# Twelve attention batches: the loop over batches written out, and two value buffers that change roles

## The reference

```
# level 0: q and k normalised per head, then rotated;  softmax over the 4096 keys
# level 1: a bias by the distance of key and query;     softmax over the 4096 keys
# level 2: softmax over the 256 queries, then each query's weights divided by their sum over the keys
k, v = heads(context @ Wk), heads(context @ Wv)          # per batch: 16 heads x 4096 x 16
att  = softmax(q @ k.T * scale (+ bias))                 # 16 heads x 256 x 4096
x    = x + (att @ v).reshape(256, 256) @ Wo
```

## Time and profile before

| | |
|---|---|
| Median of 3 runs | 7475.54 us (7468.15 to 7477.53) |
| Profiled execution, its own time | 7475.55 us |
| Its span | 7473.7 us |
| PE, DVE, ACT, POOL busy | 81%, 57%, 44%, 14% of the span |
| Mean granted TensorE clock | 0.898 |
| Instructions | 103657 |

### The profile page before, as it was taken

One profiled execution on the slowest core, in us unless ns is written; L12 is line 12 of the kernel. 1 busy time (PEld: TensorE's weight loads), 2 busy tenths in 40 slices (PEclk: granted clock), 3 DMA queues, 4 the chain that ended last, 5 costly groups with the idle time before them and its releaser, 6 DMA issues. The chain is left out here.

```text
span 7473.7 us, 103657 instructions
## 1 busy us (share of the span) xinstructions
PE 6076.2 (81%) x35500; PEld 3371.3 (45%) x35500; DVE 4251.5 (57%) x8502; ACT 3271.1 (44%) x7854; POOL 1056.2 (14%) x1131
## 2 busy tenths in 40 slices
PE   6798898979288369898898897878777898987887
PEld 3343443423155245454445554333333565556754
DVE  8677787839311236565573332888877444534631
ACT  3566565520033125454453111989889224532211
POOL 4222222004332320000000002111000000001100
PEclk8899998979599689999998998999988777998998
DMA  3323222130288433222210113322321000022100
GB/s 110 90 73 91 75 84 65 55 105 0 88 258 259 129 113 82 69 74 79 66 50 29 36 36 97 96 83 78 94 65 56 11 0 6 0 76 67 49 21 24
DMA packets 281192, 549.50 MB, mean 74 GB/s; under 512 B 29726, under 2 KB 186789, under 8 KB 261909
## 3 DMA queue, kind: packets, MB, share of 16 engines
q1 hardware_dynamic: 262388, 493.46, 22.2%
q0 software_dynamic: 18336, 50.09, 1.8%
HBM read 414.73 MB, written 128.75 MB: 73 GB/s over the span
## 5 line engine op out<-in xcount | busy, mean ns | idle before, releaser
L2413 DVE TENSOR_REDUCE t<-banks 128x1 f32<-128x512 f32 x2048 | 1373.1, 690 | 369.2 <-PE banks L2296 301.9
L2501 ACT ACTIVATE t<-banks 128x1024 f32<-128x1024 f32 x1024 | 1043.7, 1024 | 786.8 <-PE banks L2325 781.9
L2739 ACT ACTIVATE t<-banks,t 128x256 f32<-128x256 f32 x2048 | 938.1, 513 | 70.0 <-DVE t L2676 51.5
L2296 PE MATMUL banks<-t 96*128 96x512 bf16 x2048 | 798.9, 395 | 208.7 <-PEq L66 91.6
L2676 DVE TENSOR_REDUCE t<-banks 128x4 f32<-128x1024 f32 x512 | 623.7, 1219 | 92.2 <-PE banks L2622 53.0
L2342 PE MATMUL banks<-t 128*17 128x256 f32 x8192 | 642.2, 385 | 20.7 <-ACT t L2501 17.5
L2325 PE MATMUL banks<-t 97*128 97x256 bf16 x4096 | 650.6, 273 | 0.0
L2325 PEld LDWEIGHTS banks<-t 97*128 97x128 bf16 x4096 | 390.3, 98 | 256.3 <-issue 111.6
L2296 PEld LDWEIGHTS banks<-t 96*128 96x128 bf16 x2048 | 198.6, 97 | 659.7 <-DVE t L2413 336.4
L2739 ACT ACTIVATION_READ_ACCUMULATOR t<-banks,t 128x1 f32 x2048 | 494.4, 245 | 0.0
L2635 PE MATMUL banks<-t 128*17 128x256 f32 x4096 | 328.9, 407 | 160.9 <-DVE t L2687 108.1
(11 more groups left out here) (424 smaller groups left out, 10155.9 us busy)
## 6 DMA issues: line engine op xcount, KB each, us to landing
t<-in_L_ffn_w SPq DMA_DIRECT2D x127, 640.0 KB, 5.6
scratch_k<-t SPq DMA_DIRECT2D x192, 384.0 KB, 14.4
t<-scratch_k SPq DMA_DIRECT2D x192, 384.0 KB
t<-in_ctxT SPq DMA_DIRECT2D x128, 512.0 KB, 15.5
t<-scratch_k SPq DMA_DIRECT2D x192, 256.0 KB
t<-scratch_k SPq DMA_DIRECT2D x192, 128.0 KB
t<-in_L_ffn_w SPq DMA_DIRECT2D x18, 1024.0 KB
t<-in_c_rope_k SPq DMA_DIRECT2D x32, 512.0 KB, 16.6
```

The source lines that it names most:

```text
L2296: mm = nc.tensor.matmul(ps[:, 4 + g % 2, :], qstack[0:SHIFT, h, t * P:(t + 1) * P], kstack[0:SHIFT, h % 3, kc * KC:(kc + 1) * KC], start=T ...
L2413: nc.vector.tensor_reduce(gm[:, h % 2, g // NK, g % NK:g % NK + 1], ps[:, 4 + g % 2, :], AX.X, ALU.max).then_inc(max_done, 1)
L2501: nc.scalar.activation(p[:, i % 3, :].rearrange("p (b t) -> p b t", b=2), ps[:, 2 * (i % 2):2 * (i % 2) + 2, :], ACT.Exp).then_inc(exp_don ...
L2739: nc.scalar.activation(p[:, i % SL, j * T:(j + 1) * T], ps[:, 2 * (i % 3) + j // 2, (j % 2) * T:(j % 2 + 1) * T], ACT.Exp, bias=nm[:, i % ...
```

## The change

The loop is a Python loop, so that the body is emitted three times with constant batch numbers. The two buffers are a list, batch `b` reads `values[b % 2]` and fills `values[(b + 1) % 2]`, and the copy, with its part of each of the three engines, is gone from `output_product`.

```diff
-def output_product(core, att, attT, wo, b, moved=None, first=None):
+def output_product(core, att, attT, wo, b, first=None):
...
             nc.scalar.copy(attT[:, :, :], ps[:, 0:CT, 0:T]).then_inc(copied, 1)
-            if moved:
-                nc.scalar.copy(moved[1][:, CUT:CUT2], moved[0][:, CUT:CUT2])
-
-        if moved:
-            @block.gpsimd
-            def _(pool):
-                nc.gpsimd.tensor_copy(moved[1][:, CUT2:], moved[0][:, CUT2:])
 
         @block.vector
         def _(dve):
-            if moved:
-                nc.vector.tensor_copy(moved[1][:, 0:CUT], moved[0][:, 0:CUT])
             for t in range(QT):
...
-        v, v_next, kstack = sb([P, KT, H, VW]), sb([P, KT, H, VW]), sb([P, 3, S], BF16)
+        values, kstack = [sb([P, KT, H, VW]) for _ in range(2)], sb([P, 3, S], BF16)
...
-            project_first(core, wq, queries, q_rope, scale, wk, wv, context(0), keys[0], v, k_rope)
+            project_first(core, wq, queries, q_rope, scale, wk, wv, context(0), keys[0], values[0], k_rope)
...
-        of_batch = lambda b: (queries[:, :, :, bass.ds(b * T, T)].rearrange("s d h n -> (s d) h n"), keys[b], q97, k97)
+        of_batch = lambda b: (queries[:, :, :, b * T:(b + 1) * T].rearrange("s d h n -> (s d) h n"), keys[b], q97, k97)
 
         def attend_batch(b, coming):
             if by_key:
-                attend_by_key(core, keys[b], v, q97, k97, att, coming)
+                attend_by_key(core, keys[b], values[b % 2], q97, k97, att, coming)
             else:
-                attend_context(core, keys[b], v, q97, k97, tiles, att, coming)
-            output_product(core, att, attT, wo, b, (v_next, v) if coming else None, of_batch(b + 1) if coming else None)
+                attend_context(core, keys[b], values[b % 2], q97, k97, tiles, att, coming)
+            output_product(core, att, attT, wo, b, of_batch(b + 1) if coming else None)
...
-        with nc.Fori(0, B - 1) as b:
-            attend_batch(b, dict(w=wk, w_v=wv, v=v_next, source=context(b + 1), dest=keys[b + 1], rope=k_rope))
+        for b in range(B - 1):
+            attend_batch(b, dict(w=wk, w_v=wv, v=values[(b + 1) % 2], source=context(b + 1), dest=keys[b + 1],
+                                 rope=k_rope))
         attend_batch(B - 1, None)
```

More of the change, by code:

```diff
@@ L2517, in _ @@
                         new.low_parts(pool, u)
-def output_product(core, att, attT, wo, b, moved=None, first=None):
+def output_product(core, att, attT, wo, b, first=None):
     nc, ps = core.nc, core.ps
     QT = T // P
-    CUT, CUT2 = KT // 2, KT * 13 // 16
     with phase(core, "turned", "copied", "ready", "landed") as (block, turned, copied, ready, landed):
@@ L2775, in context_attention @@
             layer_norm(core, core.x, core.xn, core.xnT, loads=loads + [(wq[:, :, :], ktiles(d[prefix + "_Wq"]))],
-                       constants=[(kstack[SHIFT:ROWS, :, :], 1.0), (v[:, :, :, D:VW], 1.0), (v_next[:, :, :, D:VW], 1.0)]
+                       constants=[(kstack[SHIFT:ROWS, :, :], 1.0), (values[0][:, :, :, D:VW], 1.0),
+                                  (values[1][:, :, :, D:VW], 1.0)]
                        + ([(eps[:, :], 1e-6)] if rope else []))
-            project_first(core, wq, queries, q_rope, scale, wk, wv, context(0), keys[0], v, k_rope)
+            project_first(core, wq, queries, q_rope, scale, wk, wv, context(0), keys[0], values[0], k_rope)
         qstack, att, attT = sb([P, H, T], BF16), sb([P, T // P, C]), sb([P, CT, T])
         k97, q97 = kstack[0:ROWS], qstack[0:ROWS]
-        of_batch = lambda b: (queries[:, :, :, bass.ds(b * T, T)].rearrange("s d h n -> (s d) h n"), keys[b], q97, k97)
+        of_batch = lambda b: (queries[:, :, :, b * T:(b + 1) * T].rearrange("s d h n -> (s d) h n"), keys[b], q97, k97)
         def attend_batch(b, coming):
             if by_key:
-                attend_by_key(core, keys[b], v, q97, k97, att, coming)
+                attend_by_key(core, keys[b], values[b % 2], q97, k97, att, coming)
             else:
-                attend_context(core, keys[b], v, q97, k97, tiles, att, coming)
-            output_product(core, att, attT, wo, b, (v_next, v) if coming else None, of_batch(b + 1) if coming else None)
+                attend_context(core, keys[b], values[b % 2], q97, k97, tiles, att, coming)
+            output_product(core, att, attT, wo, b, of_batch(b + 1) if coming else None)
         with phase(core, "landed") as (block, landed):
```

## The result

The changed kernel takes 7447.66 us at the median of ten runs (7439.03 to 7456.25); the kernel before took 7468.54 beside it (ten runs, 7455.94 to 7477.53). The ratio is 0.9973, with a 95% interval of 0.9964 to 0.9982: some 20 us faster, between 13 and 27. The profiled execution took 7456.25 us, span 7454.4, and is the longest of its ten.

A forecast was written before the change was run, and what follows sets the result against it. No engine's work but transfers, then PE's taken branch, were held to set the boundaries between batches. Branches 9.0, earlier issue 3.0, last batches 0.4 and copy 0 gave 12.4 us off 7475.55: 7463, range 7451 to 7474.

The forecast's parts named there:

- The starting point: Whole kernel: the gain was taken off the profiled execution's 7475.55 us, with the median of the runs at 7475.54.
- The copy at nothing: Output phases between batches: the copy lies under the transfers, so removing it gains 0 us.
- The branches: Loop ends: nine branches go, six of them taken; batches 1 and 2 become as long as batch 0, 9.0 us won.
- give-back at level 0: Level 0 attention: PE starts sooner but waits for head 1's keys; the branch's 3.4 us shrink to 1.9 there.
- Earlier issue in the attention phases: Attention phases: constant addresses let head 1's keys go out some 0.4 us earlier, 3.0 us won over nine phases.
- The last batches: Three last batches of the attentions: they lose only SP's share of an addition and a branch, 0.4 us together.
- The register work in the output phases at nothing: Output phases: issues about 0.35 us earlier, but loading phases issuing so are not shorter; 0 us, upper end 3.2.
- The test that I had named for it: Output phases: the copy's zero, covering register work too, fails if their mean leaves 18.6 to 19.6 us.
- The signs: Signs of being right, such as attention phases of batches 1 and 2 within 1 us of batch 0's at each level.
- The whole stall comes back: Rival, loop ends: six branches at 3.386 us plus 3.4 of earlier issue, 23.7 off, 7452 us; chance 0.17.
- The transfers take it all: Rival, attention phases: the earlier start is waited off at head 1's keys, only 3.4 us left, 7472; chance 0.20.
- The collision: Rival, output phases: closer loads of queries and keys collide, 13.5 us lost there, 7480 us in all; chance 0.08.

The follow-up runs named there:

- e1: Kernel before with the loop kept and only the copy left out; 7465.18 us, ratio 1.0001 to the kernel before.
- e2: Kernel before with the loop written out (constant batch numbers) and the copy kept; 7443.61 us, ratio 0.9965 to the kernel before.
- e8: Kernel before (loop, copy, registers) with each head's keys loaded in six transfers instead of three; 7369.58 us, ratio 0.9872 to the kernel before.
- e6: Changed kernel with each head's keys loaded in six transfers of 16 rows instead of three; 7351.82 us, ratio 0.9839 to the kernel before.
- b2: Kernel before once more, unedited, for a second profile; 7467.13 us in one run.
- e7: Changed kernel put back into a loop with taken branches, all addresses constant, every pass doing batch 0, no copy; 7461.1 us, ratio 0.9991 to the kernel before.
- a2: Changed kernel once more, unedited, for its scatter and a second profile; 7446.16 us, ratio 0.9971 to the kernel before.
- e3: Changed kernel with each written-out body in a loop of one pass, so no branch is taken; 7444.42 us, ratio 0.9967 to the kernel before.

## Why the prediction was wrong in size

It missed by 15.3 us, of which two parts are to be kept apart: some 7 are the starting point, the other 8 the gain, 12.4 forecast and some 20 measured.

**The starting point, 7.0 us too high.** The forecast took its gain off a profiled execution of 7475.55, the same as the median of three runs, and held that "the same number holds" for the kernel. That lies near the top of what this kernel does: the median of ten runs, with those three among them, is 7468.54, and medians in three later sets are 7465.35, 7470.09 and 7467.21. From 7468.5 the same 12.4 us would have given 7456, and the range, moved with it, would have held the result.

**The copy at nothing: right.** e1 and e2 show it from both sides, and e8 even with the cover cut to 11 us.

**The branches, 9.0 us: the term that was mis-sized; 13.8 measured.** At level 0 they gave 7.4 instead of 4.2, at level 1 6.0 instead of 5.9, at level 2 0.4 won instead of 1.1 lost. PE begins at once, as forecast, and at levels 1 and 2 the phases lie within 2 us of each other and of the forecast. What failed is the give-back at level 0, "head 1's keys land when they land, and PE stands there instead". PE does stand there, for 0.9 to 3.2 us in the twelve batches of the four written-out profiles, but e6 shows that this wait does not lengthen the phase. What made batch 0, the model, long was 3.4 us at the lower clock behind its wait (334.6 us; 332.4 in b2 with a wait of 2.60 and no fall). The window of the kernel before, columns as in the last section:

```profile
235.40:238.80 3.40, 3.40 (x16) 1.11 (x15) 2.03 (x3) 1.58 (x2) 1.26 (x1) 0.50 0.16 64
```

At level 2 the forecast named the wrong wait: PE stands at the first context chunk, 3.11 us in the kernel before, and not at head 1's keys, 0.65.

**Earlier issue in the attention phases, 3.0 us: not seen.** e7 has the constants and the old phase lengths. The forecast's list of issues also leaves out a table that SP loads at level 0 between the first chunk and head 1's keys (line 2088). **The last batches, 0.4: not seen** (755.3 against 755.5). With these the attention phases were forecast at 12.4 and measured at 13.6 with a standard error of 2.5: the sum agrees, by two errors against each other.

**The register work in the output phases at nothing: probably too low.** "The loading phases issue just so and are not shorter" rested on three phases of 19.3 us on the mean. The same three phases in nine profiles, 27 with unchanged code, take 18.65, so those three were high by chance; single phases scatter by 0.7 to 0.9, and a mean over three cannot carry a difference of 0.4. With constants the output phases are shorter by 0.44 us each, 4.0 in all with a standard error of 1.9, near the upper end of 3.2 that the earlier issue gives by itself. The test that I had named for it, a mean outside 18.6 to 19.6, could not have shown it in the one profile after (18.84). How much of the missing 8 us lies here, and how much in the scatter of the other stages, stays open; the interval of the gain itself, 13 to 27 us, reaches down almost to the 12.4.

**The signs.** Batches 1 and 2 were to be within 1 us of batch 0 at each level. At level 1 they are; at level 0 batch 1 is 3.7 us shorter in the profile after, by the clock, while in e2 and a2 they are within 0.6; at level 2 batch 1 is 1.4 longer.

**The rivals.** "The whole stall comes back" gave 7452, and by time it lies nearest. Its price was worked out from the median of nine branches, three of which fall through; the six taken ones of the kernel before sum to 23.0 us (8.3, 7.7 and 6.9 by level). Of these 13.8 came back, nearly all at level 0, most at level 1 and next to nothing at level 2, so the rival holds by level and not as a whole. "The transfers take it all" holds at level 2 alone, and by another transfer than the one it named. The collision did not occur: output phases became shorter, not longer. The Trainium skill's page Runtime: NRT & Kernel Launch, section Instruction fetch mechanics, which was weighed for the first rival, is borne out by e3 and e7 as to the stall: 67 to 83 ns for a branch that falls through, 3.3 to 5.0 us for one that is taken. DMA queues marked "instruction" are busy in these stalls. In the first, from 569.0 to 572.4 us in the kernel before (queue, kind: packets, MB, share):

```profile
q14 instruction: 2, 0.02, 2.0%
q8 instruction: 1, 0.02, 1.8%
```

In each of the six there are three or four such packets, and in the same stretch of the changed kernel none to two. That PE waits for just these is not shown. What a stall is worth in the end the page does not say; what comes behind it decides that.

## What to carry to other kernels

What a stall at the head of a phase is worth differs from level to level of the same code. The first wait after it may take it back, as the chunk does at level 2, or may cost nothing, as the one for head 1's keys at level 0; only a run without the wait tells the two apart. A term taken as zero from a handful of rows needs their scatter beside it, and so does a baseline of three runs: here they moved the forecast by some 4 and by 7 us, where the change was worth 20. When a phase is bounded by a transfer, read the strip of the DMA engines early. Here one that stayed at a tenth or two went with a transfer whose shape, not its bytes or its order, was what to change, and that was worth five times the change under study.

## What the runs showed of the hardware that had not been expected

While the keys load in three transfers, most of the DMA engines' time is idle, and what is issued behind them lands late: the keys' 768 KB kept a phase at 19 us in three transfers, at 11 in six and at 13.4 in twelve of eight rows, and a context chunk behind them landed in 15.7 us instead of 6.2.

After a short wait TensorE sometimes ran at its lower clock. The windows of the changed kernel behind head 1's keys in the three batches of level 0 (stretch, its length, busy us of PE, PEld, DVE, ACT, POOL, granted clock, DMA share, GB/s):

```profile
232.50:239.10 6.60, 5.97 (x22) 2.38 (x23) 3.76 (x6) 2.05 (x2) 1.27 (x1) 0.50 0.15 61
589.40:596.00 6.60, 6.60 (x42) 2.92 (x41) 5.81 (x9) 4.47 (x6) 1.28 (x1) 1.00 0.15 61
939.10:945.70 6.60, 6.19 (x22) 2.51 (x23) 4.03 (x6) 2.05 (x2) 1.26 (x1) 0.50 0.16 62
```

After idling for 3.17 and 2.68 us PE was granted 0.50 (1.2 GHz) and got through 22 matmuls in the stretch; after 2.87 us it kept 1.00 (2.4 GHz) and got through 42. The two phases with the fall are 3.5 us longer than the one without (336.2 and 336.0 against 332.5), and the length of the wait doesn't tell them apart. In the other written-out profiles the clock fell behind waits of 2.85 and 2.43 us (e3: 336.3 and 335.8 us) and did not fall behind six waits of 1.5 to 2.5 (e2, a2: 332.1 to 332.7). With the keys in six there is no such wait and the phases are 332 to 334 us. What decides whether the clock falls stays open.
